# Cross layers of a graph network in 7 block products in place of 8, with the neighbour weight ahead of the adjacency

## The chip, the cores and the metric

One core of one Trainium2 chip runs the whole program in one launch. The metric is device time in microseconds, the median of the runs. TensorE (PE in the profile) multiplies, VectorE (DVE), ScalarE (ACT) and GpSimd (POOL) do the elementwise work, and SyncE (SP) issues most of the DMAs. Each engine works through its own instructions in order and waits on semaphores for the others.

## What is computed

1250 nodes have 1024 features each. Four blocks follow one another, each with a layer norm ahead and the input added back: a gated graph network of four hops, a dense layer with four low-rank paths of which a gate picks one (stage B), a graph network of two layers, and a mixture of eight experts. The change is about the third:

```python
deg_inv = 1.0 / jnp.maximum(deg, 1.0)

def _sage_layer(h, edge_src, edge_dst, deg_inv, W_self, W_neigh, b):
    msg = h[edge_src]
    agg = jax.ops.segment_sum(msg, edge_dst, num_segments=h.shape[0])
    mean = agg * deg_inv[:, None]
    return h @ W_self + mean @ W_neigh + b

h = jax.nn.relu(_sage_layer(x, ..., W_self0, W_neigh0, b0))
out = _sage_layer(h, ..., W_self1, W_neigh1, b1)
```

The inputs and the result are f32. All weights here are 1024x1024.

## The kernel before

**Tiles.** The nodes stand in ten row tiles of 125 (`NT`), features in eight blocks of 128 (`KT`). The adjacency is dense in SBUF (`adj`, f16, small whole numbers). A f32 matrix is kept as two f16 parts, high and low, where low = f32 value minus high. A dense product takes three f16 products: high by high, high by low, low by high. For one row tile that is 8 blocks x 3 x 2 halves of 512 columns = 48 matmuls (helper `wide`, L1361).

**Third block, in six stages.** `own0`: x @ W_self0 of ten tiles, 480 matmuls, weights in `wb`. `means(0)`: the adjacency by the node features `nm`, in three strips of columns, 480 matmuls (L1432); DVE multiplies each result by `dinv_row` (one over the degree, laid out along a row, L2387), ACT makes the high part (L1810), DVE the low part (L2392), which gives `tb`, already turned for the next product. `neighbours(0)`: `tb` @ W_neigh0, 480 matmuls. Then `own` (S1), `means(1)` and `neighbours(1)` for the second layer. The own products go to DRAM (`self_d`) and are loaded back as the neighbour products come. In `neighbours(1)` each tile also gets its layer norm (`stats_d`), is turned by DMA, and is routed to the experts (`route`), two tiles behind.

**Left operands.** `ln_c` (ACT, L612 and L614) and `low_c` (DVE, L604) make the two parts of the normed rows, and SP turns them with two DMA transposes for each tile (L930), 40 in stages B to S1.

**Weights.** POOL alone prepares those of the third block but the first: per block of 128 rows a load, a scaling (L718), a cast (L719) and a subtraction (L720), each of 1024 columns. This runs one or two stages ahead of its use, in 24 rounds. W_self0 is prepared during stage B, by ACT (L1792, L1793) and POOL (L823).

**Degrees.** `row_degrees` (PE) and the `dinv_row` instructions (ACT L1754, DVE L2211 and L2212) work out the inverse degrees along a row inside the gated hops. `take_degrees` has the same degrees one per node, along a column.

## Time and profile before

| | us |
|---|---|
| median of 3 runs | 1471.95 (1470.53 to 1473.56) |
| span of the profiled execution | 1469.8 |
| third block on TensorE | 587.1 to 1173.8 |
| of it the first stage, `own0`, 480 matmuls | 103.70 |
| `means(0)` and `means(1)`, 480 matmuls each | 84.63 each |
| `neighbours(0)` and `own` of layer 1, 960 matmuls | 207.20 |

The median is 2.1 us above the span of the profiled execution; terms are summed against the span and the 2.1 us is added. A chain row gives the start, the duration and the instructions that were followed back from the end. A window row gives for a stretch of time how long each engine was busy in it.

### The profile page before, as it was taken

The numbers are of one execution on the slowest core, as the hardware profiler recorded it, in microseconds if no ns is written. First come the engines' busy times: TensorE is split into PE (matmuls) and PEld (weight loads), VectorE is DVE, ScalarE is ACT, GpSimd is POOL, SyncE is SP. The second block draws the span as 40 slices with busy tenths as digits, with TensorE's granted clock in tenths as the row PEclk, the third lists the DMA queues.
The fourth block names the chain that finished last, engine by engine and source line by source line (L and its number), as shares of the span: only waits on it lengthen the run. The fifth ranks groups of instructions, "written<-read, shape, count | busy, mean of one in ns | idle before, by whom it ended". The sixth has DMA issues, their size and how long they took to land.

```text
span 1469.8 us, 28270 instructions
## 1 busy us (share of the span) xinstructions
PE 1409.7 (96%) x8327; PEld 723.4 (49%) x8327; DVE 892.5 (61%) x2053; ACT 545.3 (37%) x758; POOL 358.6 (24%) x373
## 2 busy tenths in 40 slices
PE   6889999999999999999999999999999979999996
PEld 5334454545444444444654444446444435566653
DVE  7988888686988887541542222323357775676652
ACT  4678747373524543220111220001111125565551
POOL 4331230202201210000875003700012311442232
PEclk9999999999999999999999999999999988999998
DMA  7332010000266665543323444430056646889863
GB/s 287 55 76 56 4 58 0 29 0 29 75 197 177 163 170 173 160 127 115 127 74 100 104 98 144 157 126 0 0 173 186 186 179 195 242 247 282 267 166 58
DMA packets 156675, 185.96 MB, mean 127 GB/s; under 512 B 106172, under 2 KB 107659, under 8 KB 156600
## 3 DMA queue, kind: packets, MB, share of 16 engines
q1 hardware_dynamic: 144440, 143.07, 32.0%
q0 software_dynamic: 12160, 41.95, 11.0%
q8 instruction: 40, 0.66, 0.2%
q14 instruction: 35, 0.29, 0.1%
HBM read 118.40 MB, written 41.94 MB: 109 GB/s over the span
## 4 chain that ended last, share of the span: by engine, by line
PE 74%; DVE 12%; issue 6%; ACT 3%; DMA 2%; DVEq 2%; POOL 1%; ACTq 0%; SPq 0%; POOLq 0%
PE ps L1361 30%; PE ps L1432 12%; PE ps L1596 7%; PE ps L1616 6%; PE ps L1261 3%; PE ps L1262 3%; PE ps L1263 3%; PE ps L1192 2%; PE ps L1622 1%; PE ps L1584 1%; ACT th L1700 1%; DVE hm L2085 1%; PE ps L1219 1%; DVE bstat L578 1%; PE ps L1290 1%
## 5 line engine op out<-in xcount | busy, mean ns | idle before, releaser
L1361 PE MATMUL ps<-wa,tb 128*128 128x512 f16 x960 | 208.8, 379 | 0.0
L1432 PE MATMUL ps<-adj,nm 128*128 128x384 f16 (+2 forms) x960 | 169.6, 340 | 0.0
L1261 PE MATMUL ps<-gp,hop 128*128 (+1 forms) x400 | 151.6, 379 | 1.0 <-DVE gn L2159 1.0
L1262 PE MATMUL ps<-gp,hop 128*128 (+1 forms) x400 | 151.6, 379 | 0.0
L1263 PE MATMUL ps<-gp,hop 128*128 (+1 forms) x400 | 151.6, 379 | 0.0
L1361 PEld LDWEIGHTS ps<-wa,tb 128*128 (+1 forms) x960 | 93.3, 98 | 111.4
L1432 PEld LDWEIGHTS ps<-adj,nm 128*128 x960 | 93.9, 98 | 75.4
L1810 ACT ACTIVATE tb<-cx 128x384 f32 (+1 forms) x48 | 26.8, 559 | 273.2 <-DVE cx L2387 273.2
L1361 PE MATMUL ps<-wa,hop 128*128 128x512 f16 x480 | 105.3, 379 | 2.9 <-DVEq L2334 2.9
L1596 PE MATMUL ps<-tkT,wb 128*128 128x314 f16 x768 | 106.0, 301 | 0.8 <-ACT tkT L1883 0.8
L1361 PE MATMUL ps<-wb,hop 128*128 128x512 f16 x480 | 103.8, 379 | 0.0
L1361 PE MATMUL ps<-wb,tb 128*128 128x512 f16 x480 | 103.8, 379 | 0.0
L1596 PEld LDWEIGHTS ps<-tkT,wb 128*128 128x128 f16 x768 | 75.4, 99 | 31.8 <-issue 3.8
L1616 PE MATMUL ps<-wa,hT 128*128 128x512 f16 x384 | 85.2, 379 | 1.7 <-issue 1.7
L2387 DVE TENSOR_TENSOR cx<-ps,dinv_row 128x384 f32<-128x384 f32 (+1 forms) x48 | 28.9, 602 | 94.1 <-PE ps L1432 94.1
L2090 DVE TENSOR_TENSOR hop<-hm,hop 128x640 f32 (+1 forms) x80 | 68.6, 894 | 11.5 <-ACT hop L1705 11.3
L1361 PEld LDWEIGHTS ps<-wb,hop 128*128 128x128 f16 x480 | 46.9, 98 | 56.8 <-issue 0.4
L1361 PEld LDWEIGHTS ps<-wb,tb 128*128 (+1 forms) x480 | 47.0, 98 | 56.6
L1361 PEld LDWEIGHTS ps<-wa,hop 128*128 128x128 f16 x480 | 46.2, 98 | 58.0 <-DVEq L2334 3.3
L1705 ACT ACTIVATE hop<-hm 128x640 f32 (+1 forms) x80 | 58.8, 736 | 34.2 <-DVE hm L2085 34.1
L718 POOL TENSOR_SCALAR stage<-stage 128x1024 f32<-128x1024 f32 x32 | 33.8, 1055 | 153.7 <-DVE bcur L2021 127.1
L2085 DVE SCALAR_TENSOR_TENSOR hm<-adj,th 128x640 f32<-128x640 f32 (+1 forms) x80 | 66.4, 867 | 7.3 <-ACT th L1700 5.2
(401 smaller groups left out, 2194.8 us busy)
## 6 DMA issues: line engine op xcount, KB each, us to landing
w_st<-in_ew SPq DMA_DIRECT2D x16, 2048.0 KB, 11.7
self_d<-cr SPq DMA_DIRECT2D x20, 512.0 KB, 3.0
cr<-self_d SPq DMA_DIRECT2D x20, 512.0 KB, 3.3
stage<-in_wn POOLq DMA_DIRECT2D x16, 512.0 KB, 3.8
x_d<-cr SPq DMA_DIRECT2D x10, 512.0 KB, 4.7
cx<-x_d SPq DMA_DIRECT2D x10, 512.0 KB, 4.0
cr<-x_d SPq DMA_DIRECT2D x10, 512.0 KB, 4.0
out<-cr SPq DMA_DIRECT2D x10, 512.0 KB, 3.4
```

Of the source, the lines that this page charges most:

```text
L718: link(g.tensor_scalar(st, st, SW ** 0.5, SW ** 0.5, ALU.mult, ALU.mult))
L1192: pe.matmul(ps[:, 2 + j, :], yT[:, j, part, k, :], w1[:, w, k, :], start=(n == 0), stop=(n == 3 * KT - 1))
L1261: pe.matmul(acc, wh, gh, start=(s_ == 0), stop=False, skip_group_check=True)
L1262: pe.matmul(acc, wh, gl, start=False, stop=False, skip_group_check=True)
L1263: return pe.matmul(acc, wl, gh, start=False, stop=(s_ == NT - 1), skip_group_check=True)
L1361: ins = pe.matmul(ps[:, b + c, :], lhs(part, k), w[:, w_, k, c * 512:(c + 1) * 512], start=(k == 0 and part == 0 and w_ == 0), stop=(last ...
L1432: ins = pe.matmul(ps[:, 6 + j, 0:n], nm[:, part, s_, bass.ds(f * P, P)], adj[:, s_, t0 * TP:t0 * TP + n], start=first, stop=(s_ == NT - 1 ...
L1596: ins = pe.matmul(ps[:, 2 + h, 0:FW], w1b[:, j, w_, k * H + h * P:k * H + (h + 1) * P], tkT[:, j, part, k, 0:FW], start=(k == 0 and w_ == ...
L1616: ins = pe.matmul(ps[:, 6 + (j + o) % 2, :], hT[:, part, h, c * P:(c + 1) * P], half(h, w_, o), start=(n == 0), stop=(n == len(terms) - 1))
L1705: s.activation(tile_of(hop[:, h, 0], t).rearrange("p (d n) -> p d n", n=P)[:, :, 0:TP], hm[:, j, :].rearrange("p (d n) -> p d n", n=TP), A ...
L2085: v.scalar_tensor_tensor(hm[:, j, :], tile_of(adj[:, :, h * HALF:(h + 1) * HALF], t), 2.0, th[:, j, :], ALU.mult, ALU.mult).then_inc(s_hm, 1)
L2090: v.tensor_tensor(tile_of(hop[:, h, 1], t).rearrange("p (d n) -> p d n", n=P)[:, :, 0:TP], hm[:, j, :].rearrange("p (d n) -> p d n", n=TP) ...
```

## The change

Each dense 1024x1024 product of the third block is now made for a pair of row tiles at once. The pair is a 2x2 block matrix (two row tiles, two halves of the depth), the weight is a 2x2 block matrix of 512x512, and the product is made by seven block products with sums of blocks (`PRODUCTS`), not eight. Each block product is 4 x 3 = 12 matmuls of 512 columns, 84 for a pair, against 96. The left sums are made by POOL (`sums`), the right sums (of weight blocks) by POOL, ACT and DVE (`lows_of_blocks`, `sums_high`, `weight_low`). Four passes of five pairs run: own and neighbour product of layer 0 (n = 0 to 9), then of layer 1 (n = 10 to 19). The seven left parts of a pair are turned by seven DMA transposes: 140 in all in place of 40.

The neighbour product now comes ahead of the adjacency: x @ W_neigh is evicted by ACT and DVE, split in two f16 parts (`gs`), and the adjacency is applied to it row tile by row tile (`mean_rows`, 40 matmuls of 512 columns for a tile). The inverse degree is then one number per row, applied in the eviction (`mean_out`, `out_c`), and `row_degrees` and `dinv_row` go.

Weights of pass k (8 half rounds each): k = 0 during stage B, k = 1 in the pairs 0 to 3 of pass 0, k = 2 during the means of layer 0, k = 3 in the pairs of pass 2. The first pair of layer 1 (m = 10) is prepared during the means of layer 0 too. The row tiles of the layer input are loaded by pairs (`load_pair`), once for the own and once for the neighbour pass. In the last stage POOL adds the residual (`add_rest`), tile by tile.

```diff
+PRODUCTS = (("a11", "b11"), ("s1", "t1"), ("a22", "t4"), ("s2", "t2"), ("a12", "b21"), ("s4", "b22"), ("s3", "t3"))
...
+            def lows_of_blocks(k, r, buf):
+                u, c, st = r % 2, r // 2, quads(buf, r % 2)
+                g.wait_ge(s_wh, HALF_ROUNDS * k + r + 1)
+                for right, row, o in (("b11", 0, 0), ("b21", 1, 0), ("b22", 1, 1)):
+                    g.tensor_tensor(piece(k, right, 1, c, u), st[:, row, o], piece(k, right, 0, c, u), ALU.subtract)
+                link(g.tensor_tensor(st[:, 0, 0], st[:, 0, 1], st[:, 0, 0], ALU.subtract))
+                g.tensor_tensor(st[:, 0, 1], st[:, 1, 1], st[:, 0, 1], ALU.subtract)
+                link(g.tensor_tensor(st[:, 1, 1], st[:, 1, 1], st[:, 0, 0], ALU.subtract))
+                g.tensor_tensor(st[:, 1, 0], st[:, 1, 0], st[:, 1, 1], ALU.subtract).then_inc(s_wt, 1)
...
+            def sums(m):
+                y_ = ys[m % 2]
+                left, right_ = slice(0, 512), slice(512, 1024)
+                g.wait_ge(s_lo, 4 * m + 2)
+                link(g.tensor_tensor(y_[:, 1, right_], y_[:, 1, left], y_[:, 1, right_], ALU.add))
+                g.tensor_tensor(y_[:, 1, left], y_[:, 0, left], y_[:, 1, left], ALU.subtract).then_inc(s_sum, 1)
+                link(g.tensor_tensor(y_[:, 0, left], y_[:, 1, right_], y_[:, 0, left], ALU.subtract))
+                g.tensor_tensor(y_[:, 0, right_], y_[:, 0, right_], y_[:, 0, left], ALU.subtract).then_inc(s_sum, 1)
...
+            def weights_in_pair(k, c):
+                if 1 <= c < 4:
+                    load_weights(k, 2 * c + 1, stage)
+                if c < 4:
+                    lows_of_blocks(k, 2 * c, stage)
+                    if c < 3:
+                        load_weights(k, 2 * c + 2, stage)
+                    lows_of_blocks(k, 2 * c + 1, stage)
+
+            for l in range(2):
+                if l == 0:
+                    g.wait_ge(B.mm, NT)
+                    load_weights(1, 0, stage), load_weights(1, 1, stage)
+                else:
+                    load_weights(2, 0, stage), load_weights(2, 1, stage)
+                    for r in range(HALF_ROUNDS):
+                        lows_of_blocks(2, r, stage)
+                        if r + 2 < HALF_ROUNDS:
+                            load_weights(2, r + 2, stage)
+                        if r == 3:
+                            sums(10)
+                    g.wait_ge(s_wd, HALF_ROUNDS * 3)
+                    load_weights(3, 0, stage), load_weights(3, 1, stage)
...
+                for c in range(PAIRS_N):
+                    sums(10 * l + c + 1)
+                    weights_in_pair(1 + 2 * l, c)
+                for c in range(PAIRS_N - 1):
+                    sums(10 * l + PAIRS_N + c + 1)
...
+            def load_pair(m):
+                if m >= 2:
+                    sp.wait_ge(s_lo, 4 * (m - 2) + 4)
+                i = m % PAIRS_N
+                for j in range(2):
+                    sp.wait_ge((s_B_st if m < 10 else s_hst)[j], 16 * ((i if m in range(0, 5) or m in range(10, 15) else 4) + 1))
+                    sp.dma_start(ys[m % 2][:, j, :], rows(x2_d if m < 10 else h1_d, 2 * i + j)).then_inc(s_yl[m % 2], 16)
...
+            def turn_part(m, left):
+                right = dict(PRODUCTS)[left]
+                sp.wait_ge(s_lo, 4 * m + LOWS[left])
+                if left == "a22" and m >= 2:
+                    sp.wait_ge(s_pm, DONE[m - 2, right])
+                if left != "a22" and m >= 1:
+                    sp.wait_ge(s_pm, DONE[m - 1, right])
+                sp.dma_start_transpose(slot(m, left), stg[:, AT[left]].rearrange("p a n -> p (a n)")).then_inc(s_t[left], 16)
...
-            def row_degrees():
-
-                for c in range(3):
-                    w_ = min(CC, NP - CC * c)
-                    for t in range(NT):
-                        ins = pe.matmul(ps[:, 5 + c, 0:w_], ones16[0:TP, :], adj[:, t, CC * c:CC * c + w_],
-                                        start=(t == 0), stop=(t == NT - 1))
-                ins.then_inc(s_deg, 1)
...
+            def product(n, right):
+                left = LEFT_OF[right]
+                pe.wait_ge(s_t[left], T_0[left] + 16 * (n + 1))
+                blk, acc = sets[PLACE[n // PAIRS_N]][right], ps[:, bank_of(n, right), :]
+                begins = right in ("b11", "t1", "b21")
+                for k in range(4):
+                    for part, w_ in ((0, 0), (0, 1), (1, 0)):
+                        ins = pe.matmul(acc, slot(n, left)[:, 4 * part + k, :], part_of(blk, w_)[:, k, :],
+                                        start=(begins and k == 0 and part == 0 and w_ == 0), stop=(k == 3 and part == 1),
+                                        skip_group_check=True)
+                ins.then_inc(s_pm, 1)
...
+            def mean_rows(l, t, s0, s1):
+                if s0 == 0:
+                    pe.wait_ge(s_gl, KEPT[10 * l + 8, "t4"])
+                    if l == 0 and t < 2:
+                        pe.wait_ge(B.out, NT + 2)
+                    else:
+                        pe.wait_ge(s_mo, NT * l + t - 1)
+                for s_ in range(s0, s1):
+                    if t < 2 and s_ >= NT - 2:
+                        pe.wait_ge(s_gl, KEPT[10 * l + 9, ("b22", "t4")[s_ - NT + 2]])
+                    for c in range(2):
+                        for part in range(2):
+                            ins = pe.matmul(ps[:, 2 + 2 * (t % 2) + c, :], adj[:, s_, t * TP:(t + 1) * TP],
+                                            gs[l][s_][:, part, c * 512:(c + 1) * 512], start=(s_ == 0 and part == 0),
+                                            stop=(s_ == NT - 1 and part == 1), skip_group_check=True)
+                if s1 == NT:
+                    ins.then_inc(s_mm, 1)
...
+            def blocks_high(k, c, u, buf):
+                r, st = HALF_ROUNDS * k + 2 * c + u, quads(buf, u)
+                s.wait_ge(s_wl[u], WL_0 + 32 * (HALF_ROUNDS // 2 * k + c + 1))
+                s.activation(buf[:, u], buf[:, u], ACT.Copy, scale=SW).then_inc(s_wsc, 1)
+                s.wait_ge(s_wsc, r + 1)
+                for right, row, o in (("b11", 0, 0), ("b21", 1, 0), ("b22", 1, 1)):
+                    ins = s.activation(piece(k, right, 0, c, u), st[:, row, o], ACT.Copy)
+                ins.then_inc(s_wh, 1)
+
+            def sums_high(k, c, u, buf):
+                st = quads(buf, u)
+                s.wait_ge(s_wt, HALF_ROUNDS * k + 2 * c + u + 1)
+                for right, row, o in (("t1", 0, 0), ("t3", 0, 1), ("t4", 1, 0), ("t2", 1, 1)):
+                    ins = s.activation(piece(k, right, 0, c, u), st[:, row, o], ACT.Copy)
+                ins.then_inc(s_whs, 1)
...
+            for t in range(NT):
+                relu(t)
+                if t < HALF_ROUNDS:
+                    sums_high(2, t // 2, t % 2, stage)
+                if t + 2 < HALF_ROUNDS:
+                    blocks_high(2, t // 2 + 1, t % 2, stage)
+                if t == 3:
+                    high_a(10, 0), high_a(10, 1)
+                if t == 4:
+                    high_s(10)
...
+            def pair(n, k, c):
+                m, own = n + 1, own_pass(n)
+                prep = m % 10 != 0
+                stats = n + 2 < PAIRS_N
+                if not own and n % PAIRS_N:
+                    g_low(n - 1, "t3")
+                if stats:
+                    stats_p(n + 2)
+                if own:
+                    evict(n, "b11")
+                if prep:
+                    low_a_p(m, 0), low_a_p(m, 1)
+                if own:
+                    if c:
+                        weight_low(k, c - 1, 1)
+                    evict(n, "t1")
+                if stats:
+                    coefficients_p(n + 2)
+                if n and own_pass(n - 1):
+                    evict(n - 1, "t4")
+                elif n % PAIRS_N:
+                    g_low(n - 1, "t4")
+                if prep:
+                    low_s_p(m, 1)
+                if own:
+                    evict(n, "t2")
+                if prep:
+                    low_s_p(m, 0)
+                evict(n, "b21"), evict(n, "b22")
+                if own and c < 4:
+                    weight_low(k, c, 0)
+                if not own:
+                    g_low(n, "b21")
+                evict(n, "t3")
+                if not own:
+                    g_low(n, "b22")
...
+            two_passes(0, 1)
+            for t in range(NT):
+                mean_out(t)
+                if t < HALF_ROUNDS:
+                    weight_low(2, t // 2, t % 2)
+                if t == 3:
+                    low_a_p(10, 0), low_a_p(10, 1)
+                if t == 4:
+                    low_s_p(10, 1), low_s_p(10, 0)
+            two_passes(10, 3)
```

**GpSimd, third block.** Before, a round of `means(0)`'s weight preparation (`wa` is the neighbour weight of layer 0):

```order
L712 DMA stage<-in_wn0 128x1024
L718 TENSOR_SCALAR stage<-stage 128x1024
L71 REGISTER_ALU
L719 ISA
L719 COPY wa<-stage 128x1024
L71 REGISTER_ALU
L720 ISA
L720 TENSOR_TENSOR wa<-stage,wa 128x1024
```

Now, pair n = 1 of the first own pass (`cx` holds the pair's rows, `stage` the weight blocks); the last five rows come a second time, behind another load:

```order
L966 TENSOR_TENSOR cx<-cx 128x512
L967 TENSOR_TENSOR cx<-cx 128x512
L968 TENSOR_TENSOR cx<-cx 128x512
L969 TENSOR_TENSOR cx<-cx 128x512
L942 DMA stage<-in_wn0 128x2x256 x2
L949 TENSOR_TENSOR wa<-stage,wa 128x256 x3
L950 TENSOR_TENSOR stage<-stage 128x256
L951 TENSOR_TENSOR stage<-stage 128x256
L952 TENSOR_TENSOR stage<-stage 128x256
L953 TENSOR_TENSOR stage<-stage 128x256
```

POOL had nothing to do in `own0`; now it has 18 TENSOR_TENSORs and two double loads in each of the pairs 0 to 3, and the left sums of a pair stand in the same queue as the weights.

**VectorE, first own pass.** Before, one tile of `own0` behind its statistics (`nm` is the low part of the left operand, `cr` the evicted product):

```order
L604 ISA
L604 TENSOR_TENSOR nm<-cy,nm 128x1024
L2357 ISA
L2367 SCALAR_TENSOR_TENSOR cr<-ps,bias 128x512 x2
L71 REGISTER_ALU
```

Now, from the eviction of b11 to the second half of the weight lows of the same pair (n = 3; `stg` holds the low parts of the left blocks and sums):

```order
L2711 SCALAR_TENSOR_TENSOR cr<-ps,bias 128x512
L2675 TENSOR_TENSOR stg<-yb1,stg 128x2x512
L2678 TENSOR_TENSOR stg<-yb1,stg 128x512
L2690 TENSOR_TENSOR wa<-stage,wa 128x256
L2690 TENSOR_TENSOR cy<-stage,half1 128x256
L2690 TENSOR_TENSOR half3<-stage,half0 128x256
L2690 TENSOR_TENSOR blk15<-stage,blk15 128x256
L2711 SCALAR_TENSOR_TENSOR cr<-ps,bias 128x512 x2
L2683 TENSOR_TENSOR stg<-yb1,stg 128x2x512
L2711 SCALAR_TENSOR_TENSOR cr<-ps,bias 128x512
L2683 TENSOR_TENSOR stg<-yb1,stg 128x2x512
L2711 SCALAR_TENSOR_TENSOR cr<-ps,cr 128x512 x3
```

Between the evictions stand four low parts of left operands and, in most own pairs, two groups of four weight lows; each waits for ACT, and that for POOL.

**VectorE, means of layer 0.** Before, one round of a strip:

```order
L2387 TENSOR_TENSOR cx<-ps,dinv_row 128x384
L2384 REGISTER_ALU
L2387 TENSOR_TENSOR cx<-ps,dinv_row 128x384
L2391 REGISTER_ALU
L2392 ISA
L2392 TENSOR_TENSOR tb<-cx,tb 128x384
```

Now, the evictions of tiles 3 and 4 with what stands between them:

```order
L2776 SCALAR_TENSOR_TENSOR cr<-ps,dinv,cr 128x512 x2
L2690 TENSOR_TENSOR wa<-stage,wa 128x256
L2690 TENSOR_TENSOR cy<-stage,half1 128x256
L2690 TENSOR_TENSOR half3<-stage,half0 128x256
L2690 TENSOR_TENSOR blk15<-stage,blk15 128x256
L2675 TENSOR_TENSOR stg<-cx,stg 128x2x512
L2678 TENSOR_TENSOR stg<-cx,stg 128x512
L2776 SCALAR_TENSOR_TENSOR cr<-ps,dinv,cr 128x512 x2
```

The eviction of a tile of the means now stands behind a weight round, and that of tile 4 behind the first parts of pair 10 as well.

## Rows read from the trace of the kernel before

**Rows 1.** The page: busy time of each engine, share of the span, instructions.

```profile
PE 1409.7 (96%) x8327; PEld 723.4 (49%) x8327; DVE 892.5 (61%) x2053; ACT 545.3 (37%) x758; POOL 358.6 (24%) x373
```

**Rows 2.** The chain that ended last, third block: start us, us, what.

```profile
587.13 103.70 PE ps L1361 x480
690.83 84.63 PE ps L1432 x480
...
982.66 84.63 PE ps L1432 x480
...
1098.76 10.38 PE ps L1361 x48
1109.52 10.38 PE ps L1361 x48
```

**Rows 3.** Windows: stretch, its us, engines' busy us, granted clock, DMA share, GB/s.

```profile
587.00:691.00 104.00, 104.00 (x484) 47.18 (x484) 41.63 (x105) 18.38 (x16) 0.00 (x0) 1.00 0.46 129
691.00:775.00 84.00, 84.00 (x478) 46.67 (x477) 39.40 (x47) 12.78 (x23) 63.09 (x53) 1.00 0.34 113
879.00:983.00 104.00, 104.00 (x485) 47.18 (x484) 27.10 (x31) 2.12 (x2) 40.13 (x32) 1.00 0.40 136
```

**Rows 4.** The same chain in the gated hops, where the inverse degrees stand.

```profile
172.15 1.23 ACT dinv_row L1754 x3
...
381.65 2.16 DVE dinv_row L2211
```

**Rows 5.** Timeline of VectorE at the start of `own0`: statistics and low part.

```profile
588.67 2.47 DVE L578 BATCH_NORM_STATS2 bstat<-cx 128x6 f32<-128x512 f32 x4 [0.22 <-DVE cr L2331]
...
596.41 1.23 DVE L604 TENSOR_TENSOR nm<-cy,nm 128x1024 f16<-128x1024 f32 x1 [2.40 <-ACT nm L614]
```

**Rows 6.** DMA issues: transfer, count, size, median us from issue to landing.

```profile
stage<-in_wn POOLq DMA_DIRECT2D x16, 512.0 KB, 3.8
...
cx<-x_d SPq DMA_DIRECT2D x10, 512.0 KB, 4.0
...
tb<-nm SPq DMA_TRANSPOSE x20, 3.2
```

**Rows 7.** Single lines' durations, ns min/median/max, first and last start.

```profile
L747 POOL TENSOR_TENSOR xt<-xt,gn x10: 1264/1284/1409, 44.8 to 144.5; 128x512 f32<-128x512 f32 x10
...
L870 POOL TENSOR_TENSOR tot<-tot,tokg x2: 355/356/357, 1188.7 to 1189.5; 128x80 f32<-128x80 f32 x2
...
L614 ACT ACTIVATE nm<-cy x10: 1056/1056/1057, 564.6 to 662.1; 128x1024 f32 x6, 128x1024 f16<-128x1024 f32 x4
...
L930 SPq DMA_TRANSPOSE tb<-nm x20: 1232/1243/1344, 791.1 to 885.3; - x20
```

**Rows 8.** Timeline of `means(0)`: GpSimd and VectorE beside each other.

```profile
701.70 0.59 POOL L712 DMA_DIRECT2D stage<-in_wn  x1 [0.75 <-POOL wa L720]
...
704.82 2.21 POOL L720 TENSOR_TENSOR wa<-stage,wa 128x1024 f32 x1 [0.19 <-POOL wa L719]
705.27 2.17 DVE L2392 TENSOR_TENSOR tb<-cx,tb 128x384 f32 x1 [0.23 <-ACT tb L1810]
...
710.87 2.50 POOL L720 TENSOR_TENSOR wa<-stage,wa 128x1024 f32 x1 [0.18 <-POOL wa L719]
```

**Rows 9.** Groups by form, 691 to 775: busy us, mean ns, idle before.

```profile
L2392 DVE TENSOR_TENSOR tb<-cx,tb 128x384 f32 x16 | 18.6, 1184 | 1.5 <-ACT tb L1810 1.5
L2387 DVE TENSOR_TENSOR cx<-ps,dinv_row 128x384 f32<-128x384 f32 x16 | 8.9, 555 | 24.7 <-PE ps L1432 24.7
```

**Rows 10.** The same groups, 983 to 1067, where GpSimd rests.

```profile
L2387 DVE TENSOR_TENSOR cx<-ps,dinv_row 128x384 f32<-128x384 f32 x16 | 8.9, 558 | 30.7 <-PE ps L1432 30.7
L2392 DVE TENSOR_TENSOR tb<-cx,tb 128x384 f32 x16 | 8.8, 552 | 3.7 <-ACT tb L1810 3.7
```

**Rows 11.** Windows of the first stage: one before a wait of TensorE, one behind.

```profile
63.70:69.10 5.40, 5.36 (x31) 2.54 (x32) 5.40 (x12) 4.72 (x10) 3.13 (x3) 1.00 0.13 49
75.40:82.50 7.10, 7.08 (x32) 2.99 (x33) 5.12 (x18) 3.85 (x9) 0.00 (x0) 0.76 0.47 106
```

756 lines of the change are left out of this document (471 added, 285 removed).

## Prediction

> **What bounds the kernel now.** I read the page first: TensorE is busy in 96% of the span [rows 1]. Then the chain that ended last: the third block is one unbroken run of matmuls, 103.70 us for the 480 of `own0` and 84.63 us for each of the two adjacency stages [rows 2], with nothing of another engine between them. Then the windows, stage by stage: TensorE is busy in all of 104 and 84 us at full granted clock, while VectorE has 41.63, 39.40 and 27.10 us of work and GpSimd 0, 63.09 and 40.13 [rows 3]. So the third block is bound by TensorE alone, until the last stage, where a tile of 10.38 us comes every 10.76 us [rows 2]. Fewer matmuls are worth their full time as long as the other engines stay hidden. They get much more to do in less time, so the question is how long their work takes in each new stage.
>
> **The change: TensorE.** A matmul of 512 columns costs 103.70 / 480 = 0.216 us [rows 2]. The twenty pairs have 1680 of them in place of 1920: -240 x 0.216 = -51.8 us. The adjacency takes 400 of 512 columns for a layer, 86.4 us, against 84.63: +3.5 us for both. A pair now has 84 x 0.216 = 18.1 us; all that one pair needs from others has to fit there.
>
> **Degrees.** `dinv_row` lies on the chain with 1.23 and 2.16 us [rows 4], but in each place another engine's work is nearly as late. I take 2.0 us, between nothing and the 3.4 of the two rows. Sum so far: -51.8 + 3.5 - 2.0 = **-50.3 us**.
>
> **First pair.** The second pair of rows (m = 2) is loaded only after the last store of stage B, and its statistics stand ahead of the eviction of the first product in VectorE's queue. The last eviction of stage B ends near 588.5 (the next row starts at 588.67 [rows 5]); store and load take about 4 each [rows 6], behind 5 other issues on SP; statistics 2.47 [rows 5]. So the product that waits for that eviction starts at 597 to 602 in place of 592.3: +5.3 to +10; I take +8.5.
>
> **Own pairs, GpSimd.** In each of the pairs 0 to 3 of an own pass GpSimd has, in order: four sums of 512 columns, 1.28 each [rows 7], with two gaps of 0.19 [rows 8] = 5.5; a double load issue, 1.2 [rows 8]; seven subtractions of 256 columns; a second issue, 1.2; seven more. No row has 256 columns: between 0.36 for 80 and 1.28 for 512 [rows 7] a straight line gives 0.73, so 5.1 for seven. Ahead of the second issue it waits until ACT has made four high parts (a quarter of 1.06 each [rows 7], 1.1) and VectorE four low parts (0.55 for 384 columns [rows 10], so some 0.36 for 256, 1.45). With 0.1 for semaphores: 5.5 + 1.2 + 5.1 + 2.65 + 1.2 + 5.1 = 20.7 us in a pair of 18.1. The sums of the next pair stand behind all this in one queue, and TensorE needs them: GpSimd becomes the bound, +2.6 us for each pair.
>
> **Own pairs, VectorE beside GpSimd.** The timeline of `means(0)` shows a subtraction of VectorE, started at 705.27 under one of GpSimd that ran from 704.82 to 707.03, take 2.17 us, until 0.41 behind GpSimd's end [rows 8]. By form: 1184 ns for it with GpSimd busy in 75% of the stretch, 552 with GpSimd at rest; while the multiplication that reads PSUM takes 555 and 558 [rows 9, 10]. GpSimd pays too: one subtraction took 2.50 in place of 2.21 [rows 8]. So a subtraction with both inputs in SBUF and GpSimd's work go one after the other. An own pair has four such of VectorE for the left parts: three of 1.23 [rows 5] and one of half the columns, 4.4 us, less the gaps of GpSimd (4 x 0.19), three quarters of it under work: +2.7. The weight lows come later behind delayed ones, about +1.0 (one blocked step of half a GpSimd operation for each of two groups). Cycle 24.4, +6.3 for a pair. One of the eight pairs is paid by what the first sums are early: 7 x 6.3 = **+44 us**. Ends: 7 x 2.6 = 18 with no blocking; 8 x 7.5 = 60 if every such step collides.
>
> This mechanism stands in the Trainium skill too ("SBUF — State Buffer", Who interferes with whom): VectorE operations with two SBUF inputs share a port pair with GpSimd's reads, as an exclusive lock. By that rule the trace agrees, 1184 against 552 ns; without the lock the sum would have 18 here, with it all the way 60.
>
> **DMA.** A pair moves 3.15 MB and seven transposes. From 879 to 983 the DMA engines were busy 0.40 x 104 = 41.6 us for 136 GB/s x 104 us = 14.1 MB [rows 3], 2.95 us per MB; a transpose adds 1.2 to 1.4. That is 18 to 19.5 us in a pair of 24.4: hidden, but near the bound if GpSimd were not late. SP issues a transpose in 1.24 [rows 7], 8.7 for seven, and lands it in 3.2 [rows 6].
>
> **Second layer's start.** The eviction of the first product of pass 2 waits for the last store of the hidden rows: +3 us (0 to 5).
>
> **Means of layer 0.** ACT has in order, for each tile: relu 0.9, sum highs 1.05, then block highs 1.9 of the next but one weight round. That waits for its load, 3.8 from issue to landing [rows 6] and 1.0 for the issue of two, which waits for the weight lows, 1.45. The ring closes: 4.8 + 1.9 + 0.9 + 1.05 + 1.45 + 0.3 for semaphores = 10.4 us for a tile, against 40 x 0.216 = 8.64 on TensorE. The evictions of the means stand in VectorE's queue behind these lows, and that of tile 4 also behind the left parts of pair 10, some 11 us behind the lows of round 3. With the first lows at +23 us and 10.4 each, those are at +54, and tile 4 is evicted at +65 where TensorE would want it at +54.5; tile 5, behind the next left parts and GpSimd's sums for pair 10 (5.5) and subtractions (5.1), another 14 late. I take **+25 us** (10 to 30).
>
> **Last stage.** The first routing waits for the chain from tile 0's eviction to its transposes: 32 us where 28.5 are there, +3.3; GpSimd has a residual addition of 2.2 us more in each 9-us tile. +6 us (3 to 20).
>
> **Clock.** In the first stage, behind a wait of TensorE, the granted clock of 7.1 us was 0.76, and 32 matmuls took 7.08 us where 31 had taken 5.36 at 1.00 [rows 11]: 1.7 us for a long stall; I count three, +5 (0 to 8).
>
> **Sum.** -50.3 + 8.5 + 44 + 3 + 25 + 6 + 5 = +41.2; 1469.8 + 41.2 + 2.1 outside the span = **1513 us**.
>
> **Rivals.**
> - **GpSimd keeps up**, so faster. If subtractions of 256 columns cost near the 80-column 0.36, a cycle is 5.5 + 2.4 + 5.0 + 2.65 = 15.6 and fits in 18.1 even with part of the blocking. The own pairs cost nothing, the ring of the means, which has little of GpSimd, 15: -50.3 + 6 + 0 + 2 + 15 + 3 + 3 = -21.3, 1451 us. It decides at 0.55 us for each subtraction. Against it: 1.28 for 512 columns.
> - **No blocking**, only GpSimd's order: -50.3 + 8.5 + 18 + 3 + 22 + 6 + 4 = +11.2, 1483 us. Against it stand 1184 and 552 ns [rows 9, 10]; for it, that GpSimd itself lost only some tenths.
> - **Blocking in full, or DMA-bound own pairs**: 60 in place of 44, and 8 more in neighbour pairs, whose left parts meet GpSimd's sums: 1537 us. By the skill's rule (an exclusive lock for a whole instruction) this is what would come out if nearly every step collided; the rows bear it out for single steps.
> - **The work is not reduced**: a pair might need other matmuls than I count. The order of both kernels shows 12 for each product; nothing for this one.
>
> **How the numbers follow.** The forecast 0.45; GpSimd keeps up 0.13; no blocking 0.2; full blocking or DMA 0.2; the rest spread. The range takes in from the better half of the faster rival's neighbourhood, 1468, up to 1545, which leaves out about 2 in 10, most of it below. A measurement of this kernel can tell 0.2%, 3 us. Faster by more 0.14, within 0.05, slower 0.81.
>
> **What would show it.** Right: a pair of the first own pass lasts 24 to 25 us in the windows, a neighbour pair 18 to 20; GpSimd busy in over 80% of own pairs, TensorE waiting there for transposes whose sources were late from GpSimd's sums; subtractions L2675, L2683 of 1.23 us at rest take up to 2.5; the means of layer 0 over 100 us with waits for `mean_out`; the experts' part unchanged. Wrong: own pairs of 18 to 19 us, or GpSimd's 256-column step at 0.4 us. What would overturn the sum from outside it: a longer stage B, where the weights of pass 0 are now prepared, or a stage of the experts that loads later.

## The result, and the profile after

The changed kernel took 1584.62 us in the median of four runs, the kernel before 1472.28 in the same session: a ratio of 1.0752, with a 95% interval of 1.0730 to 1.0773. One of the four runs took 2063.9 us at a granted clock of 0.654 and is left out of the ratio; the others took 1580.1, 1584.5 and 1584.7. It is slower by 112 us, where I had forecast slower by 41. The profiled execution had a span of 1583.1 us (1584.74 with what lies around it) at a granted clock of 0.951. Against the 1469.8 of before that is 113.3 us, and the stages below add up to it.

The page of the changed kernel, busy time of each engine and, further down, the shares of the chain that ended last:

```profile
PE 1400.1 (88%) x7897; PEld 689.3 (44%) x7897; DVE 1028.2 (65%) x2197; ACT 715.2 (45%) x1097; POOL 586.7 (37%) x671
...
PE 47%; DVE 19%; DMA 9%; POOL 8%; issue 7%; ACT 5%; SPq 3%; DVEq 1%; ACTq 0%; POOLq 0%
```

TensorE has fewer instructions than in [rows 1] and is now idle for 12% of a longer span; VectorE, ACT and GpSimd have all gained work. What TensorE waited for from 580 to 1300 us (total, times, longest):

```profile
PE ps L1627 <- DVE cr L2711: 66.6, 17, 9.4
PE ps L1670 <- DVE cr L2776: 28.8, 3, 13.2
PE ps L1711 <- issue: 10.4, 5, 4.8
```

The first is a product of a pair (L1627) that waits until VectorE's eviction (L2711) has emptied its PSUM tile: 17 waits, up to 9.4 us. The second is the adjacency's matmul (L1670), which waits in the same way for `mean_out` (L2776). Where the chain of before was one run of matmuls [rows 2], there is now a wait of that kind in nearly every own pair. The windows (length, then busy time of TensorE, weight loads, VectorE, ACT and GpSimd, then granted clock, DMA share, GB/s):

```profile
441.00:587.00 146.00, 135.43 (x707) 67.75 (x706) 125.02 (x422) 80.26 (x126) 76.69 (x107) 0.99 0.56 164
587.00:627.00 40.00, 22.90 (x81) 8.41 (x79) 29.38 (x63) 12.71 (x20) 13.77 (x16) 0.79 0.75 146
...
742.00:834.00 92.00, 90.92 (x423) 41.06 (x421) 40.94 (x50) 42.74 (x59) 27.51 (x20) 1.00 0.68 150
834.00:951.00 117.00, 88.15 (x380) 38.03 (x379) 29.42 (x52) 39.11 (x78) 51.77 (x72) 0.87 0.44 137
...
971.00:1075.00 104.00, 81.52 (x341) 34.54 (x340) 67.49 (x80) 40.35 (x78) 80.59 (x86) 0.92 0.81 184
```

The neighbour pass of layer 0 (742 to 834) is as full as [rows 3] was. The first pair (587 to 627) has TensorE busy for 22.90 of 40 us, at clock 0.79. In four pairs of the second own pass (971 to 1075) GpSimd is busy in 80.59 of 104 us and no engine in all of it: that is no engine short of throughput, but a ring of engines that wait for each other.

Cut by TensorE's first matmul of each stage, this is where the 113 us are. "At 0.216" is the number of the stage's matmuls by the price of [rows 2].

| stage | before | after | at 0.216 | above it |
|---|---|---|---|---|
| own and neighbour pairs, layer 0 | 103.7 + 103.6 | 150.9 + 91.9 | 178.8 | +64.0 |
| adjacency, layer 0 (`means`) | 84.6 | 124.2 | 89.0 | +35.2 |
| own and neighbour pairs, layer 1 | 103.6 + 106.5 (with routing) | 120.0 + 92.5 | 178.8 | +33.7 |
| adjacency, layer 1 | 84.6 | 114.6 (with routing) | 89.0 | +25.6, 2.8 of it there before |
| stage B, own weights of layer 0 now beside it | 145.7 | 152.8 | | +7.1 |
| up to stage B (hops) | 441.4 | 438.2 | | -3.2 |
| from the experts on | 296.0 | 298.1 | | +2.1 |

64.0 + 35.2 + 33.7 + 22.8 + 7.1 - 3.2 + 2.1 = 161.7, less the 48.3 that the matmuls give back, is 113.4. I call the four passes of pairs pass 0 (own) and 1 (neighbour) of layer 0, 2 and 3 of layer 1. In the runs below that leave a pass and what comes before it untouched, pass 0 took 145 to 151 us and pass 2 119 to 122 (116 to 125 where the adjacency ahead of it was changed), so a few us of such a stage are no finding. Most variants were run once. They are compared with 1584.7; since the changed kernel's own runs went from 1580.1 to 1584.7, a total that differs by 5 us shows nothing by itself. The kernel before beside them took 1471 to 1477 in the median.

### The profile page after: what moved, and what is told of

Read it like the earlier page. It is cut to its first block, busy times and chain, and to the rows that moved or that the text cites. A ratio compares the mean times of both kernels' runs of the same rounds, so it can differ in the third digit from the quotient of the medians.

```text
span 1583.1 us, 26003 instructions
## 1 busy us (share of the span) xinstructions
PE 1400.1 (88%) x7897; PEld 689.3 (44%) x7897; DVE 1028.2 (65%) x2197; ACT 715.2 (45%) x1097; POOL 586.7 (37%) x671
## 4 chain that ended last, share of the span: by engine, by line
PE 47%; DVE 19%; DMA 9%; POOL 8%; issue 7%; ACT 5%; SPq 3%; DVEq 1%; ACTq 0%; POOLq 0%
PE ps L1828 7%; PE ps L1475 6%; PE ps L1477 5%; PE ps L1476 5%; PE ps L1848 5%; DMA ring_b<-stg 5%; PE ps L1627 5%; PE ps L1574 3%; PE ps L1670 2%; SPq L1206 2%; PE ps L1415 2%; DVE stg L2683 2%; DMA stage<-in_ws 2%; POOL wb L949 1%; PE ps L1854 1%
## 5 line engine op out<-in xcount | busy, mean ns | idle before, releaser
L1627 PE MATMUL ps<-blk,ring_b 128*128 128x512 f16 x360 | 90.3, 404 | 23.6 <-DVE cr L2711 23.5
L1828 PE MATMUL ps<-tkT,wb 128*128 128x314 f16 x768 | 106.5, 302 | 0.8 <-ACT tkT L2204 0.8
L1670 PE MATMUL ps<-wb,adj 128*128 128x512 f16 x320 | 76.4, 400 | 28.8 <-DVE cr L2776 28.8
L1627 PE MATMUL ps<-wa,ring_b 128*128 128x512 f16 x240 | 61.2, 414 | 19.6 <-DVE cr L2711 19.6
L1627 PE MATMUL ps<-wb,ring_b 128*128 128x512 f16 x240 | 60.1, 409 | 20.5 <-DVE cr L2711 17.7
L1670 PE MATMUL ps<-wa,adj 128*128 128x512 f16 x320 | 75.4, 396 | 3.2 <-DVEq L2809 3.2
L1068 POOL DMA_INDIRECT out<-yb,sidx x24 | 56.8, 2366 | 56.1 <-ACT yb L2223 49.2
L1060 POOL DMA_INDIRECT gx<-h_d,idx x24 | 23.1, 960 | 137.8 <-DVE idx L2959 107.5
L1627 PEld LDWEIGHTS ps<-blk,ring_b 128*128 128x128 f16 x360 | 36.5, 103 | 73.5 <-DVE cr L2711 26.6
L1670 PEld LDWEIGHTS ps<-wb,adj 128*128 128x128 f16 x320 | 32.3, 102 | 72.0 <-issue 38.7
L1932 ACT ACTIVATE th<-arow,bcur 128x640 f32<-128x640 f32 x80 | 61.8, 814 | 1.5 <-ACT arow L1926 1.4
L1475 PEld LDWEIGHTS ps<-gp,hop 128*128 (+1 forms) x400 | 39.5, 99 | 51.2 <-issue 5.5
```

Source lines behind the costliest of these rows:

```text
L1475: pe.matmul(acc, wh, gh, start=(s_ == 0), stop=False, skip_group_check=True)
L1627: ins = pe.matmul(acc, slot(n, left)[:, 4 * part + k, :], part_of(blk, w_)[:, k, :], start=(begins and k == 0 and part == 0 and w_ == 0), ...
L1670: ins = pe.matmul(ps[:, 2 + 2 * (t % 2) + c, :], adj[:, s_, t * TP:(t + 1) * TP], gs[l][s_][:, part, c * 512:(c + 1) * 512], start=(s_ == ...
L1828: ins = pe.matmul(ps[:, 2 + h, 0:FW], w1b[:, j, w_, k * H + h * P:k * H + (h + 1) * P], tkT[:, j, part, k, 0:FW], start=(k == 0 and w_ == ...
L1932: s.activation(th[:, j, :], arow[:, h * HALF:(h + 1) * HALF], ACT.Tanh, bias=bcur[:, bass.ds(t, 1)] if not isinstance(t, int) else bcur[:, ...
```

## Experiments on the own pairs

GpSimd's timeline in the second own pass of the changed kernel (start, duration; in brackets the idle time before and what ended it):

```profile
984.08 1.92 POOL L949 TENSOR_TENSOR wb<-stage,wb 128x256 f16<-128x256 f32 x3
...
990.25 1.26 POOL L966 TENSOR_TENSOR cx<-cx 128x512 f32<-128x512 f32 x1
...
997.35 1.44 POOL L942 DMA_DIRECT2D stage<-in_wn  x2 [1.68 <-issue]
...
1003.84 0.73 POOL L953 TENSOR_TENSOR stage<-stage 128x256 f32<-128x256 f32 x1
...
1007.69 1.44 POOL L942 DMA_DIRECT2D stage<-in_wn  x2 [3.13 <-DVE blk L2690]
...
1015.33 1.26 POOL L966 TENSOR_TENSOR yb<-yb 128x512 f32<-128x512 f32 x1
...
1023.13 3.60 POOL L949 TENSOR_TENSOR wb<-stage,wb 128x256 f16<-128x256 f32 x3
...
1040.60 1.27 POOL L966 TENSOR_TENSOR cx<-cx 128x512 f32<-128x512 f32 x1
```

L966 is the first sum of a pair. It starts at 990.25, 1015.33 and 1040.60: a cycle of 25.1 and 25.3 us, where I had predicted 24.4. It is made of the parts that I had named, sums, load issue, seven subtractions of 256 columns, a wait for VectorE's weight lows, issue, seven more, and a step alone has about the price I had taken (0.66 to 0.73 for 256 columns, 1.27 for 512). In the first of the two cycles the sums take 5.4 us, the issues 2.9, the fourteen subtractions 12.0, the wait for the weight lows 3.1, and a wait ahead of the first issue, which I had not named, 1.7. GpSimd works or issues for 20.3 us of 25.1. The other side of the hand-over, just ahead of TensorE's wait:

```profile
990.33 0.42 ACT L2028 ACTIVATE wb<-stage 128x256 f16<-128x256 f32 x1 [4.11 <-POOL stage L953]
...
991.69 1.45 DVE L2690 TENSOR_TENSOR wb<-stage,wb 128x256 f16<-128x256 f32 x1 [3.47 <-ACT blk L2028]
993.07 3.22 DVE L2690 TENSOR_TENSOR blk<-stage,blk 128x256 f16<-128x256 f32 x3
996.22 1.27 DVE L2711 SCALAR_TENSOR_TENSOR cr<-ps,bias 128x512 f32<-128x512 f32 x2
996.95 3.60 PE L1627 MATMUL ps<-wa,ring_b 128*128 128x512 f16 x8 [6.03 <-DVE cr L2711]
```

GpSimd's last subtraction frees ACT, ACT's copies free VectorE's four weight lows (L2690), of which each takes more than 1 us while GpSimd's sums run (418 ns in the median of the 40 of this form), and behind them in VectorE's queue stands the eviction (L2711) that TensorE has waited 6.03 us for. My theory: **GpSimd's queue is the ring's longest arc**. The rivals: the DMA engines; the transposes, which ACT's waits name; VectorE's order, which decides who waits for whom; and the granted clock.

**The DMA engines and the weights.** `no_wdma` leaves out the loads of six of the eight half rounds of neighbour weights in each own pass (`k` is 1 and 3 there); `no_weights` leaves out those loads and all of their preparation on GpSimd and VectorE, ACT copying in its place.

```
+                if k in (1, 3) and r >= 2:
+                    g.sem_inc(s_fake[u], 1)
+                    return
```

and in `no_weights` besides, here on GpSimd:

```
                 g.wait_ge(s_wh, HALF_ROUNDS * k + r + 1)
+                if k in (1, 3):
+                    g.sem_inc(s_wt, 1)
+                    return
```

> Left out: the loads of 6 of the 8 half rounds of the weights of the first neighbour pass and of the second one (12 half rounds of 512 KB); the arithmetic is done on what lies in the buffers. All waits stand. If DMA traffic is what makes transposes and pair loads late, own pairs with weights get 3 to 6 us shorter, 20 to 35 us in all. If GpSimd's order of work is the bound, only its issues go, 1.44 us for each half round, 15 us in all at most.

> Left out: the whole preparation of the weights of the two neighbour passes on GpSimd and VectorE and 6 of 8 of its loads; ScalarE only copies what lies in the buffer, in 14 steps for a half round. All waits stand. G: the own pairs come down to 18 to 20 us, since GpSimd has only 5.5 us of sums for a pair: 75 us less in all. D: transposes still stand behind the 1 MB load, pairs stay at 22 to 25 us: 35 to 45 us less.

`no_wdma` took 1560.7 us: pass 0 at 134.6 in place of 150.9, pass 2 at 113.3 in place of 120.0. `no_weights` took 1534.6, between what its two theories had asked for: pass 0 at 114.1, pass 2 at 101.2, its pairs 18.1, 20.8, 21.1, 20.8, 20.4. The loads are worth a third to a half of what `no_weights` gains in a pass, the work on the two engines the rest. They include their issue on GpSimd, six of 1.44 us in a pass: that alone covers pass 2's 6.7 us, but not pass 0's 16.3. So in pass 0 the traffic itself counts, and the DMA engines are not ruled out there. Neither run tells GpSimd's share of the work from VectorE's. VectorE's left-part subtractions L2683 (L2700 in `no_weights`) from 950 to 1075, by form (total, mean ns, idle before), first of the changed kernel, then of `no_weights`:

```profile
L2683 DVE TENSOR_TENSOR stg<-cx,stg 128x1024 f16<-128x1024 f32 x4 | 7.7, 1933 | 0.0
L2683 DVE TENSOR_TENSOR stg<-yb,stg 128x1024 f16<-128x1024 f32 x6 | 8.0, 1341 | 4.6 <-ACT stg L2063 4.6
```

```profile
L2700 DVE TENSOR_TENSOR stg<-cx,stg 128x1024 f16<-128x1024 f32 x6 | 7.3, 1225 | 11.4 <-ACT stg L2080 11.4
```

With GpSimd's weight work gone, all twelve steps take 1225 ns. Beside it the ten of the changed kernel took 1205 to 3342 ns: five were not held up at all, and the 1933 is the mean of four, of which one took 3342. The loss is 0.35 us a step in the mean of the ten. Even so a pair of `no_weights` takes 20.8 and not 18.1: own pairs have 2.7 us beyond the weights.

**GpSimd's sums on VectorE.** `sums_vector` leaves nothing out and moves the four sums of each pair but the first to VectorE, behind the two left parts that they follow.

```
                 if prep:
-                    low_a_p(m, 0), low_a_p(m, 1)
+                    low_a_p(m, 0), low_a_p(m, 1), sums_v(m)
```

> One edit in the changed kernel: VectorE makes the sums of the left blocks (four steps of 512 columns for a pair), not GpSimd; GpSimd has only the weights left. G (GpSimd's queue, with sums and weight blocks one behind the other, sets the own pairs): the pairs with weights of pass 2 (101.6 us for four) lose most of GpSimd's 5.5 us each, to 19 to 21 us a pair, and pass 0 as much: 30 to 45 us in all, less VectorE's 3 us. If VectorE's queue and its blocking are the bound, its 3 us more for a pair make the pairs longer: 10 to 25 us slower.

1562.6 us, 22 less where the theory asked for 30 to 45; pass 2 at 109.3, pairs 21.2, 20.2, 24.7, 23.1, 20.3; pass 0 at 142.0. Taking 5.4 us a pair from GpSimd shortened pass 2 by 11, though VectorE, 65% busy on the page, got them. So work on GpSimd, or its hand-over to and from VectorE, which went with it, is on the path; about half of the time came back elsewhere in the ring.

**More work for GpSimd.** `pool_plus` adds to each of the pairs 0 to 3 five clears of an unused tile, 2.1 us:

```
+                    for _ in range(5):
+                        link(g.memset(pad[:], 0.0))
                     lows_of_blocks(k, 2 * c, stage)
```

> One edit in the changed kernel: GpSimd writes zeros five times into 328 columns that nobody reads, ahead of the weight blocks in each of the pairs 0 to 3 of both own passes; it reads nothing. The four pairs with weights of pass 2 took 101.6 us. If GpSimd's queue sets their length, they grow by the full time of the five steps (2 to 3 us a pair, 8 to 12 us for the four). If VectorE's queue sets it and GpSimd has slack, by less than a third of it.

It took 1573.3 us, not longer but shorter: pass 2 at 122.6 (+2.6), pass 0 at 137.1 in place of 145 to 151. By the test that I had set, growth by less than a third of the added time, GpSimd has slack. Its timeline says otherwise:

```profile
977.48 1.27 POOL L966 TENSOR_TENSOR cx<-cx 128x512 f32<-128x512 f32 x1
...
986.02 2.10 POOL L989 MEMSET to<- 128x328 f32 x5
988.20 1.92 POOL L949 TENSOR_TENSOR wb<-stage,wb 128x256 f16<-128x256 f32 x3
...
1003.84 1.27 POOL L966 TENSOR_TENSOR yb<-yb 128x512 f32<-128x512 f32 x1
...
1011.62 2.10 POOL L989 MEMSET to<- 128x328 f32 x5
...
1029.47 1.27 POOL L966 TENSOR_TENSOR cx<-cx 128x512 f32<-128x512 f32 x1
```

The cycle is 26.4 and 25.6 us, up by 1.3 and 0.3, not by 2.1. The three subtractions L949 behind the clears take 1.92 us; in the changed kernel they took 3.60 in that place (1023.13 above), since VectorE's left parts ran beside them. The clears fill just that time, and are not held themselves (366 to 385 ns each in all forty, 2.10 for five with their gaps); VectorE's left parts beside them take 1208 to 1214 ns, so they don't hold it up either. So GpSimd loses to VectorE too: 1.7 us of that cycle is blocking, which a step that reads nothing doesn't suffer. That pass 0 got shorter by 7 us or more I read in the same way, but did not trace step by step.

**The transposes.** ACT's waits name them: in the changed kernel its high parts (L2053) waited 60.4 us for transposes of the pair before, whose two-part issue at 595.97 (below) held SP's queue for 10.55 us, right behind a 1 MB load. `load_late` puts that load behind the pair's transposes.

```
                     turn_part(m, "s1"), turn_part(m, "s2")
-                    if m % 10 < 8:
-                        load_pair(m + 2)
...
                     turn_part(m, "s3")
+                    if m % 10 < 8:
+                        load_pair(m + 2)
```

> One edit in the changed kernel: SyncE issues the load of a later pair's rows (1 MB) behind the last transpose of the pair being prepared (s3), not ahead of those of a12, s4 and s3; the same for the first such load. Theory D (transposes behind a load in SyncE's queue): in the changed kernel the transposes behind that load took 5 to 10.6 us to issue for two, and the next high parts on ScalarE waited for them 60.4 us in all. They then land in 3 to 5 us, the own pairs of pass 0 and 2 lose 5 to 8 us each, the program 35 to 50 us. Theory G (GpSimd's queue of sums and weight blocks sets the pair, as predicted): the transposes are late because the sums are, nothing goes but the issue, at most 5 us in all.

ACT's waits from 587 to 1170 us, first of the changed kernel, then of `load_late`:

```profile
ACT stg L2053 <- DMA ring_b<-stg: 60.4, 15, 13.9
```

```profile
ACT stg L2053 <- DMA ring_b<-stg: 10.2, 4, 5.4
```

50 us of ACT's waiting is gone, and the time is 1591.8 us, pass 0 at 154.8, pass 2 at 120.3. The theory had asked for 35 to 50 us less. The edit also makes the statistics wait for a later load, which `both_late` below takes out. The longest wait in the table of that engine was off the path.

**VectorE's order.** `evict_first` puts two evictions ahead of the weight lows and of one left part.

```
                 if own:
+                    evict(n, "t1")
                     if c:
                         weight_low(k, c - 1, 1)
-                    evict(n, "t1")
```

> One edit in the changed kernel: in VectorE's queue of an own pair the eviction of t1 stands ahead of the second weight lows, and that of t2 ahead of the low parts of the sums. In the changed kernel TensorE waited 66.6 us in 17 waits for just these evictions (6.0 us at 990.9 to 997.0), each of which stood behind a step that waited for ScalarE and GpSimd. Theory Q (the order of VectorE's queue ties TensorE to the weight preparation): the waits go, pass 2 comes from 119 to 100 to 106 us, pass 0 from 146 to 125 to 133, 30 to 40 us in all. Theory P (the preparation itself, its hand-overs between GpSimd, ScalarE and VectorE, is too long for a pair): the waits come back at the transposes, passes 0 and 2 lose less than 10 us together.

1594.8 us, where the theory had asked for 30 to 40 less; pass 2 at 121.4, pass 0 at 150.0. TensorE gets one PSUM tile earlier and waits as long for the next: from 955 to 1080 us its waits for evictions are 23.1 us in eleven pieces, where they were 23.4 in seven. As I read it, the weight lows that now come later hold GpSimd's second issue, so the wait has only moved along the ring; that step was not traced.

**The clock.** In pairs 1 and 2 of pass 0, 84 matmuls took 22.2 us of TensorE's time at a granted clock of 0.84 to 0.85, in pairs 1 to 3 of pass 2 19.9 to 21.4 at 0.88 to 0.93, against 18.1 to 18.6 at full clock. `filler_own` gives TensorE 16 more matmuls, whose product is used nowhere, in each waiting place.

```
                 product(n, "b21")
+                if own_pass(n) and n % PAIRS_N < 4:
+                    filler(16)
                 evicted(pe, n, "t1")
```

> One edit in the changed kernel: TensorE runs 16 idle matmuls (3.5 us, into a bank that nobody reads) in the pairs 0 to 3 of the own passes, where it waits 4 to 6 us for the eviction of t1. In these pairs 84 matmuls took 21.9 to 22.2 us of TensorE's time where 18.1 is the full clock's, at a granted clock of 0.83 to 0.85. If the lower clock lengthens the chain, the products behind the waits take 2.6 us again and the own passes lose 2 us a pair, 16 us in all. If it only fills waits, nothing changes, within 5 us.

1580.0 us, clock 0.959, pass 2 at 121.6: no gain beyond 5 us. The pairs 1 to 3 of pass 2 of `filler_own`:

```profile
974.00:1048.00 74.00, 65.44 (x300) 28.53 (x299) 49.06 (x57) 30.69 (x60) 59.35 (x65) 1.00 0.84 199
```

The clock there is 1.00 (0.91 from 976 to 1054 in the changed kernel), the 84 matmuls of a product pair take 18.5 to 18.8 us, and the pass is no shorter. So where the path of this kernel leads through other engines, TensorE's clock costs next to nothing.

**Where this leaves the ring.** Taking work off GpSimd shortens the own passes; the transposes' issue, the order of two evictions and the clock do not. The loads count in pass 0. How much of a cycle is GpSimd's queue and how much VectorE's steps in its path stays unseparated: of 25.1 us GpSimd is idle for 4.8, most of it behind VectorE's weight lows.

## Experiments on the first pair, the means and the last stage

**First pair and the statistics.** The timeline around the first product of the changed kernel that waits:

```profile
594.28 1.65 SPq L1197 DMA_DIRECT2D cx<-x_d  x2
595.97 10.55 SPq L1206 DMA_TRANSPOSE ring_b<-stg  x2
...
596.05 0.16 DVE L2665 TENSOR_TENSOR lnv<-lnv 128x2 f32<-128x2 f32 x1
...
606.78 2.47 DVE L2654 BATCH_NORM_STATS2 bstat<-cx 128x6 f32<-128x512 f32 x4 [8.74 <-DMA cx<-x_d]
609.29 0.69 DVE L2711 SCALAR_TENSOR_TENSOR cr<-ps,bias 128x512 f32<-128x512 f32 x1
...
610.04 4.39 PE L1627 MATMUL ps<-blk,ring_b 128*128 128x512 f16 x12 [9.45 <-DVE cr L2711]
...
679.63 0.55 DVE L2665 TENSOR_TENSOR lnv<-lnv 128x2 f32<-128x2 f32 x1
```

The load of m = 2 is issued at 594.28 and lands at 606.7, after 12 us and not 4; the statistics wait 8.74 us for it, the eviction stands behind them, and TensorE behind that. At the time GpSimd's first weight loads (1 MB, issued from 591.4) and a store were in flight too, and took 5 to 11 us. Pairs 1 and 2 of pass 0 repeat the delay in small (pairs 3 and 4 have no statistics): the fifteen steps of the coefficients, of two columns each, take 0.16 us with GpSimd at rest (596.05) and mostly 0.55 or more beside it (679.63). `coef_late` moves both behind the pair's left parts:

```
-                if stats:
-                    stats_p(n + 2)
...
-                if stats:
-                    coefficients_p(n + 2)
...
                     low_s_p(m, 0)
+                if stats:
+                    stats_p(n + 2), coefficients_p(n + 2)
```

> One edit in the changed kernel: VectorE makes the statistics and the 15 small coefficient steps of a later pair (pairs 0 to 2 of pass 0) behind the low parts of the sums, not ahead of the eviction of the first product and of those low parts. Expected by the view that VectorE's queue holds back evictions: the first pair's 9.4 us wait for the eviction of b11 goes (the statistics behind a load that landed 12 us after its issue no longer stand ahead of it), pairs 1 and 2 get 3 to 5 us shorter: 15 to 20 us in all. By D alone: the first wait is only moved, 5 us or less.

1565.2 us, 19.5 less; pass 0 at 128.0, its pairs 23.5, 28.8, 27.5, 27.1, 21.1 where they were 36.1, 31.2, 34.3, 26.6, 22.8. Pass 2, which has no statistics, stayed at 119.4. That settles where most of pass 0's surplus over pass 2 came from: 12.6 us in the first pair, whose wait for the load is gone, and 9 in the next two. `both_late`, with `load_late` on top, shows that the load's place adds nothing:

> load_late and coef_late together. load_late alone cut the wait of the high parts for transposes from 60.4 to 10.2 us, yet pass 0 got no shorter (153 us against 150), since the statistics, first in VectorE's queue, then waited for the later load. If that is why, both edits together give pass 0 what either lacks: under coef_late's 127 us, 110 to 118. If the transposes never were on the path, it stays at 127.

1566.9 us, pass 0 at 127.2.

**Means of layer 0.** TensorE in three of the ten tiles, each of 32 matmuls or 8.7 us:

```profile
883.02 8.74 PE L1670 MATMUL ps<-wb,adj 128*128 128x512 f16 x32 [3.31 <-DVE cr L2776]
...
906.64 8.87 PE L1670 MATMUL ps<-wb,adj 128*128 128x512 f16 x32 [13.15 <-DVE cr L2776]
...
929.62 9.32 PE L1670 MATMUL ps<-wb,adj 128*128 128x512 f16 x32 [12.38 <-DVE cr L2776]
```

and VectorE ahead of the second wait:

```profile
903.34 1.22 DVE L2675 TENSOR_TENSOR stg<-cx,stg 128x1024 f16<-128x1024 f32 x1 [10.84 <-ACT stg L2053]
905.09 1.40 DVE L2776 SCALAR_TENSOR_TENSOR cr<-ps,dinv,cr 128x512 f32<-128x512 f32 x2
```

VectorE stood still for 10.84 us with tile 4's eviction ready behind a left part of pair 10, whose high part ACT had yet to write. `prep10_late` moves all preparation of pair 10 behind the means; `means_first` keeps it there, but puts each eviction ahead of a weight low and pair 10's parts one tile later; `no_w2` leaves out the preparation of the second layer's own weights (their loads and their parts on all engines). VectorE's part of `means_first`:

```
-                if t < HALF_ROUNDS:
-                    weight_low(2, t // 2, t % 2)
-                if t == 3:
-                    low_a_p(10, 0), low_a_p(10, 1)
+                if 1 <= t <= HALF_ROUNDS:
+                    weight_low(2, (t - 1) // 2, (t - 1) % 2)
                 if t == 4:
+                    low_a_p(10, 0), low_a_p(10, 1)
```

> One edit in the changed kernel: the left parts of pair 10 (high and low parts, sums, transposes) are made behind the means of layer 0 on every engine, not in their midst. My prediction gave the means +25 us, of them 10.8 and 14.5 at the evictions of tiles 4 and 5, behind these parts. If so the means come down from 124.2 to 95 to 105 us, and what is now behind them, some 15 to 20 us, stands between them and pass 2. If the ring of the weights (10.4 us a tile) is the cause, the means stay over 115 us and all of the later work is added.

> One edit in the changed kernel: in the first means VectorE evicts tile t+1 ahead of the weight lows of round t, the parts of pair 10 stand one tile later, and ScalarE makes relu of tile t+1 ahead of the block highs of round t+2. Without the weights the means took 88.9 us (their 412 matmuls at full clock), with them 124.2. Q: 95 to 105 us. P (eight rounds of a ring of over 10 us are too long for the means): they stay over 115, or pass 2 starts later by as much.

> Left out in the changed kernel: the preparation of the second layer's own weights on all engines and its loads, during the first means; pass 2 multiplies by the weights of pass 1. All waits stand. The means took 124.2 us against 89.0 of matmuls, and 118.2 with the parts of pair 10 behind them (of which 8.1 a wait for these parts). If the ring of the weights through VectorE's queue is the cause, the means come down to 90 to 95. If the parts of pair 10 and the round trip of the rows through DRAM are, they stay over 105.

Means 0 took 118.2 us in `prep10_late` (8.1 of it a wait for pair 10 at the end, and 124.6 in pass 2 in place of 120.0, so nothing was won: 1579.1 us in all), 111.8 in `means_first` (1565.9 in all), between its two theories, and 89.0 in `no_w2` (1550.8). 89.0 is the 412 matmuls at 0.216: the ring of the weights is the whole of the 35 us, and pair 10's parts cost only because they stand in it. A third of it, 12.4 us, could be taken back by order.

**Last stage.** The chain of the changed kernel, in order of time:

```profile
1206.62 1.42 DVE cr L2806 x2
...
1218.54 5.82 issue
1224.36 1.41 DVE cr L2806 x2
...
1236.09 1.41 DVE cr L2806 x2
...
1245.83 1.41 DVE cr L2806 x2
```

L2806 is a tile's eviction. Between 1206.62 and 1224.36 lie 17.7 us: the "issue" of 5.82 is the first expert's weights, one step of VectorE over 4096 columns:

```profile
L2875 DVE SCALAR_TENSOR_TENSOR wb<-w_st,wb x1: 6062/6062/6062, 1218.4 to 1218.4; 128x4096 f16<-128x4096 f32 x1
```

`w1_late` runs it behind the last stage.

```
+            def tail_w1():
+                tail()
+                first_weight_low()
+
-            chained(step.loop, [(out_c, 0), (stats_d, 0), (route, 2)], tail, 2 * (1 + LINKS + 3), early=first_low, then=first_weight_low)
+            chained(step.loop, [(out_c, 0), (stats_d, 0), (route, 2)], tail_w1, 2 * (1 + LINKS + 3), early=first_low)
```

> One edit in the changed kernel: VectorE makes the low part of the first expert's weights (6.1 us, 4096 columns) behind its part of the last routing, not between the evictions of tiles 2 and 3 of the second means, which stood 17.7 us apart where later ones stand 9.7 apart. If that step holds TensorE up, the last stage (114.6 us from the first matmul of the second means to the last) loses 6 to 8 us and the experts start no later. If what follows on VectorE's queue (9.7 us a tile, over TensorE's 9.0) is the bound anyway, it also loses them; if the loads of the tiles are, nothing changes.

The stage took 105.8 us in place of 114.6, but the rest 301.5 in place of 298.1, and the whole 1580.0, a total that one of the changed kernel's own runs has too: of 8.8 us, 3.4 came back at the experts. VectorE's evictions in `w1_late`:

```profile
1218.03 1.42 DVE cr L2806 x2
...
1227.80 1.41 DVE cr L2806 x2
```

9.8 us apart, as the last two above (1236.09, 1245.83), against 8.64 of TensorE for the tile's 40 matmuls. In four such tiles, 39.0 us, VectorE is busy for 31.6; of the rest 0.83 us a tile are a wait for ACT, the others small gaps between some twenty steps. So I read what is left above 89.0 as VectorE's own sequence for a tile. No run shortens that sequence, so this stands on the trace alone.

**All together.** `all_fixes` is `coef_late`, `sums_vector`, `prep10_late` and `w1_late`; `all3` is `coef_late`, `evict_first`, `means_first` and `w1_late`; `all2` is `all3` with `sums_vector`. Nothing is left out in them.

> Four edits of earlier runs together in the changed kernel: statistics and coefficients behind the low parts of the sums (alone 19.5 us less), sums of left blocks on VectorE (22), the parts of pair 10 behind the first means (5.5), the first expert's weights low behind the last routing (4.7). Nothing is left out. If they act on stages of their own, 45 to 52 us less than 1584.6: 1532 to 1540, still 4% slower than the kernel before. If the two edits on VectorE's queue meet, it stays over 1545.

> evict_first, means_first, statistics and coefficients late, the first expert's weights late, together; nothing left out. Q: 30 to 40 and 20 us off besides 19.5 and 4.7: 1500 to 1512 us. P: 1545 to 1555.

> As all3, and VectorE makes the sums of the left blocks. Alone that gave 22 us. With VectorE's evictions no longer behind GpSimd's work it should give less, 5 to 15 us over all3: 1490 to 1505 under Q, 2% slower than the kernel before; under P 1530, as with the four fixes before.

`all_fixes` took 1536.3 us in the median of four, ratio to before 1.0466 (1.0427 to 1.0505), as its first theory had it; `all3` 1540.7 in one run, far from Q's 1500 to 1512; `all2` 1522.9 in the median of four, ratio 1.0334 (1.0313 to 1.0356), nearer to P's 1530 than to Q. `all2` by stages: pass 0 117.8, pass 1 99.5, means 0 103.6, pass 2 110.4, pass 3 92.8, last 107.6. TensorE's waits in it, from 587 to 1300 us:

```profile
PE ps L1622 <- DVE cr L2717: 33.4, 16, 5.6
PE ps L1665 <- DVE cr L2778: 7.9, 2, 5.4
```

Of the 66.6 and 28.8 us 33.4 and 7.9 are left. Reordering, and moving the sums to VectorE, took back 62 of the 112 us; the change still doesn't pay. The twenty pairs cost TensorE 51.8 us less, and the ten own pairs of `all2` alone take 51.9 us more than their matmuls at 0.216 (176.3).

## Why the prediction was wrong in size

- **The nominal part held**: 51.8 - 3.5 us fewer. `no_w2`'s means at 89.0 and pass 1's 91.9 (90.7 for its 420 matmuls at 0.216) show TensorE's price unchanged. **Hops** -3.2 for -2.0: held, though the hops of the other runs took 0.7 to 3.3 us less than the one trace of before.
- **Own pairs, the cycle**: its length held in pass 2, 25.1 and 25.3 for 24.4, in part by luck. I had 20.7 us of GpSimd's own and 3.7 of VectorE's held-up steps, 2.7 in the left parts and 1.0 in the weight lows. In the four pairs from 971 to 1075 the left parts lost 1.6 us a pair and the weight lows 3.2, and some 2 and 3 us of the two cycles are GpSimd's own subtractions held up, to which I gave no price. In pass 0 the pairs 1 to 3 took 31.2, 34.3 and 26.6. That each holds the other up was shown: VectorE's step of 1024 columns up to 3342 against 1225 ns, GpSimd's three of 256 columns 3.60 against 1.92 us. The page of the Trainium skill that I weighed ("SBUF — State Buffer", Who interferes with whom) has a VectorE step with two SBUF inputs and a GpSimd step that reads SBUF lock each other out, not one that only writes it. The traces agree: 3342 and 3.60 above, and clears of 366 to 385 ns. The path that I had named did not hold: I had TensorE wait for transposes whose sources were late, but it waited 66.6 us for evictions in VectorE's queue and 5.1 for transposes.
- **First pair, +8.5 predicted: the largest miss.** The step that failed is "store and load take about 4 each". The load took 12, beside the stores, weight loads and transposes of 75% busy DMA engines, and the product that waits for the eviction started at 610.0 in place of 597 to 602. The pair took 36.1 us, 20.5 above its 72 matmuls at 0.216. I had also forgotten that the statistics and coefficients stand in the pairs 1 and 2 of pass 0 too, on the engine that GpSimd blocks, in front of an eviction. The sum for layer 0 (8.5 + 22 = 30.5) came out at 64.0; `coef_late` takes 23 of the surplus away, `no_weights` 37.
- **Pass 2 and 3, 3 + 22 predicted**, measured 33.7, of it 31.9 in the own pass (408 matmuls) and 1.8 in the other (420). I had given the neighbour pairs nothing (full blocking: 8), which is right to 2 us a pass. What is missing lies in the own pass: the cycle is 0.8 longer, and the second pair took 29.1 us.
- **Means 0, +25 predicted, +35.2 measured.** The ring of weights was the right mechanism, as `no_w2` shows, and so was tile 4's eviction behind the left parts of pair 10. The step that was mis-sized is "10.4 each" with the two late tiles that follow from it: VectorE's weight lows begin at 855.85, 866.83, 880.13 and 891.08, so the first three rounds took 11.0, 13.3 and 11.0 us, with loads that landed after up to 6.7 us where I had 3.8; the fourth, around the parts of pair 10, took 25.6. The waits are 3.31, 13.15 and 12.38 us, 29 in all, and matmuls at a granted clock of 0.87 make up the rest. The ends, 10 to 30, didn't hold it.
- **Last stage, +6 predicted, +22.8 measured**. The step that failed: I costed the routing's chain and GpSimd's addition, not VectorE's own time for a tile, 9.8 us against 8.64, and overlooked that the first expert's weights (4.42 us before, 6.06 now) were hidden before by a tile of 10.4 and are not now. `w1_late` shows the second to be worth 8.8 us of the stage.
- **Stage B, 0 predicted, +7.1 measured.** I named it as what would overturn the sum, and gave it no price. GpSimd's busy time there went from 21.5 to 76.7 us. The same step of VectorE in the stage, first before, then after, and TensorE's longest row of waits from 441 to 591 us after:

```profile
L597 DVE SCALAR_TENSOR_TENSOR lnv<-lnv 128x2 f32<-128x2 f32 x15 | 2.4, 161 | 0.5
```

```profile
L721 DVE SCALAR_TENSOR_TENSOR lnv<-lnv 128x2 f32<-128x2 f32 x10 | 3.3, 334 | 0.3
```

```profile
PE ps L1613 <- DVE zT L2638: 9.3, 4, 3.0
```

Before, TensorE waited 4.6 us for `zcat` and `zT`, VectorE's steps in the same place. That fits blocking, but no run took GpSimd's work out of the stage, so the cause is argued only.
- **Clock +5**: not a term of its own. It showed in the traces (0.84 to 0.85 in pass 0) and `filler_own` put its worth below 5 us; by counting it I had mixed a symptom into the sum.
- **The rivals.** "GpSimd keeps up" and "no blocking" fell: 0.66 to 0.73 us for 256 columns, and VectorE's steps of up to 3342 ns. "Blocking in full, or DMA-bound" would have had 1537; the pairs 2 to 4 of pass 2 are near 24 to 25 us each, so most of the excess isn't there either, but in the steps above: what I had treated as single events (a load, a chain of tiny steps, one long step) each stood at the head of a queue on the path.

Of the terms for stages that could be measured, all but the nominal part and the hops were too small. The errors went one way and didn't cancel; the range had been built as if they would.

What stays open: stage B's +7.1, why `pool_plus` shortened pass 0 by 7 us or more, why the load in the first pair took 12 us, what the DMA traffic costs in pass 0, and how GpSimd and VectorE share the length of a cycle.

## What to carry to other kernels

When the bound leaves one engine and becomes a ring of in-order queues, price for every hand-over what stands first in the waiting engine's queue, tiny steps and waits for loads included; an instruction that was free under a full TensorE is paid in full there. Test such a ring by taking work out, not by the longest row of waits (60 us of ACT's were worth nothing) nor by adding work (of 2.1 us more on GpSimd 0.8 and 1.8 were absorbed by what it was blocked for). Taking matmuls from an engine that bounds the kernel at 96% pays only if the added work of the others fits beside it with their interference, not by their busy shares.

## What the runs showed of the hardware

- Nine of fifteen steps of VectorE of two columns, all reading SBUF alone, took 0.55 to 0.69 us in place of 0.16 while GpSimd worked without gaps; the fifteen took 6.9 us (678.77 to 685.67) in place of 2.7 (595.33 to 598.05). Ten steps of 1024 columns lost 0.35 us each in the mean (0 to 2.1, against 1225 ns). The loss did not grow with the size of the step, so small ones suffer most.
- GpSimd's steps are held by VectorE's as well: three of 256 columns 3.60 us in place of 1.92. Clears in the same place, which read nothing, took 366 to 385 ns each, and VectorE's steps of 1024 columns beside them took 1208 to 1214.
- A pair of transposes issued right behind a 1 MB load held SP's queue for 10.55 us, and those of 587 to 770 us into `ring_b` landed after 5.5 us in the median (3.4 and 3.1 into `ring_a` and `ring_c`), where 3.2 were seen before [rows 6].
- 84 matmuls with waits between them took 22.2 us at a granted clock of 0.84 to 0.85. More matmuls in the waits brought the clock of three pairs of pass 2 from 0.91 to 1.00 and the mean from 0.951 to 0.959, and won no time there.
